# Shares of 24 and 8 token tiles instead of 16 and 16, and the results of six token groups loaded behind block 30 and summed between the last sends

## What is computed

```python
x = layernorm(x + attention(x))          # x: 16 x 256 tokens of 128; 16 heads of 8
x = layernorm(x + moe(x))
def moe(xf):                             # 4096 tokens
    shared = gelu(xf @ Wfc_s + bfc_s) @ Wproj_s + bproj_s      # hidden 512
    probs = softmax(xf @ Wr)             # 8 experts
    p, i = top_k(probs, 2); p = p / sum(p)
    routed = sum over the two: (gelu(xf @ Wfc[e] + bfc[e]) @ Wproj[e] + bproj[e]) * p
    return shared + routed
```

## Time and profile before

| what | us |
|---|---|
| median of three runs (590.12, 590.47, 601.82) | 590.47 |
| the profiled execution, its own time | 595.96 |
| its span, first to last instruction | 594.2 |
| attention part, up to | 279 |
| shared expert with routing and slot sends, up to | 403 |
| blocks 0 to 38, last result send ends at | 554.8 |
| sums, moments, normalisation, writing out, up to | 594.2 |

### The profile page before, as it was taken

The page is one execution under the profiler, slowest core; times in us unless marked ns, Lnnn a source line. Parts: engine busy times, 40 slices in busy tenths (PEclk is TensorE's granted clock), DMA queues, the critical chain, the costliest instruction groups (busy, mean ns, idle before and its releaser), DMA issues.

```text
span 594.2 us, 13730 instructions
## 1 busy us (share of the span) xinstructions
PE 436.2 (73%) x4871; PEld 280.8 (47%) x4871; DVE 364.2 (61%) x783; ACT 330.6 (56%) x624; POOL 327.2 (55%) x433
## 2 busy tenths in 40 slices
PE   5999999999999999984514530588989898897000
PEld 2344545555555554542303320367877687776000
DVE  3658887878787878762414710565666575664292
ACT  1148887878788888741424410564655565554043
POOL 5312676565666867437771677001655486675493
PEclk9889999999999999995756965799999999999555
DMA  3224535363645452011113111910111111000542
GB/s 89 65 63 119 154 101 154 111 156 100 174 143 154 135 145 66 30 37 40 54 54 95 34 54 54 242 34 1 38 40 35 38 36 31 30 26 29 191 160 73
DMA packets 63109, 50.25 MB, mean 85 GB/s; under 512 B 7338, under 2 KB 54580, under 8 KB 63044
## 3 DMA queue, kind: packets, MB, share of 16 engines
q1 hardware_dynamic: 58500, 40.91, 24.2%
q0 software_dynamic: 4544, 8.47, 4.3%
HBM read 24.96 MB, written 22.95 MB: 81 GB/s over the span
## 4 chain that ended last, share of the span: by engine, by line
PE 17%; another core or an unknown queue 13%; DVE 8%; ACT 6%; issue 5%; DMA 1%; POOL 1%; ACTq 0%; DVEq 0%; POOLq 0%; SPq 0%
ACT hid L1635 3%; PE h_ps L1565 2%; PE y_ps L1585 2%; PE h_ps L1566 2%; PE h_ps L1567 2%; PE y_ps L1586 2%; PE y_ps L1584 2%; ACT hid L1622 2%; DVE hid L1687 1%; DVE stats L1738 1%; DVE x_all L1735 1%; DVE var_eps L1743 1%; PE t_ps L1554 1%; ACT hid L1627 1%
## 5 line engine op out<-in xcount | busy, mean ns | idle before, releaser
L553 DVE TENSOR_REDUCE row_max<-s_ps 128x2 f32<-128x512 f32 x256 | 164.9, 683 | 49.8 <-PE s_ps L684 47.9
L413 ACT ACTIVATE probs<-ring_ps 128x1024 f32<-128x1024 f32 x128 | 130.9, 1023 | 49.0 <-PE ring_ps L702 48.6
L1481 POOL DMA_INDIRECT results<-gated,rows_in x78 | 89.8, 1151 | 93.3 <-ACT gated L1643 77.6
L684 PE MATMUL s_ps<-qk_stack 24*128 24x256 f16 x512 | 84.0, 272 | 7.8 <-DVE row_max L553 2.6
L702 PE MATMUL ring_ps<-qk_stack 26*128 26x256 f16 x512 | 83.0, 271 | 0.0
L1334 POOL DMA_INDIRECT slots<-rows,slot_at x64 | 63.7, 995 | 34.3 <-issue 19.2
L1635 ACT ACTIVATE hid<-h_ps,bias 128x256 f32<-128x256 f32 x156 | 61.3, 480 | 32.8 <-PE h_ps L1567 20.0
L720 PE MATMUL av_ps<-probs,v_aug 128*32 128x256 f32 x1024 | 68.5, 385 | 0.0
L684 PEld LDWEIGHTS s_ps<-qk_stack 24*128 24x128 f16 x512 | 34.3, 92 | 62.3 <-issue 32.8
L1585 PE MATMUL y_ps<-w,hid 128*128 x312 | 59.5, 220 | 1.7 <-issue 1.6
L1622 ACT ACTIVATE hid<-h_ps,b_units 128x512 f32<-128x512 f32 x32 | 21.9, 685 | 69.5 <-remote 59.3
(11 more groups left out here) (209 smaller groups left out, 1034.9 us busy)
## 6 DMA issues: line engine op xcount, KB each, us to landing
qk_stack<-qk_rows SPq DMA_DIRECT2D x64, 96.0 KB
slots<-empty_row SPq DMA_DIRECT2D x13, 390.0 KB, 5.2
qk_rows<-qk_parts SPq DMA_DIRECT2D x16, 256.0 KB, 2.6
rows<-results SPq DMA_DIRECT2D x8, 512.0 KB, 6.8
rows_in<-slots SPq DMA_DIRECT2D x3, 1300.0 KB, 10.8
w_stage<-in_w_fc SPq DMA_DIRECT2D x9, 256.0 KB, 3.3
w_stage<-in_w_proj SPq DMA_DIRECT2D x9, 256.0 KB, 3.8
x_t<-in_x_t SPq DMA_DIRECT2D x16, 128.0 KB, 2.2
```

Source lines behind the costliest of these rows:

```text
L413: nc.scalar.activation(probs[:, n % PROBS], ring(key), ACT.Exp, scale=SCORE_SCALE).then_inc(ring_emptied, 1)
L553: nc.vector.tensor_reduce(row_max[:, h], s1_ps[:, h % 2], AX_X, ALU.max, negate=True).then_inc(max_done, 1)
L684: mm = nc.tensor.matmul(s1_ps[:, h % 2, t], band_of(q_stack, b, h, TERM_ROWS)[:, t * P:(t + 1) * P], band_of(k_stack, b, h, TERM_ROWS), st ...
L1481: nc.gpsimd.indirect_dma_start(out=a["results"][:, :], out_offset=bass.IndirectOffsetOnAxis(ap=rows_in[:, 2 * n + half, DEST:DEST + 1].bit ...
```

## The change

The shares become 24 and 8 tiles. With them the Placer sends 48 rows of tiles for the first share and 16 for the second; the blocks that are surely full are 17 instead of 9, and the first share's tokens lie in blocks 0 to 30 (`EARLY_BLOCKS` = 31). Eleven of the thirteen emptying DMAs, not eight, are waited for ahead of the first share (`FIRST_TILES` 66). SP waits for the sends of blocks 0 to 30 and loads the results of groups 0 to 5, then waits for all and loads those of groups 6 and 7. POOL sums group g behind its sends of block 33 + g. Behind the last send and the sixth sum it takes one inverse root over the 24 columns of six groups, and then works on groups 6 and 7 as before. VectorE, behind its last block, takes the moments of groups 0 to 5, makes their six shifts, and then goes on with groups 6 and 7.

```diff
@@ -30,7 +30,7 @@
-SHARES = ((0, 16), (16, 32))
+SHARES = ((0, 24), (24, 32))
@@ -897,8 +897,11 @@
-FIRST_TILES = 48
+FIRST_TILES = 66
 FULL_BLOCKS = TOP * SHARES[0][1] // 2 - (EXPERTS - 1)
+EARLY_BLOCKS = TOP * SHARES[0][1] // 2 + EXPERTS - 1
+EARLY_GROUPS = SHARES[0][1] // GROUP
+SUM_AT = {EARLY_BLOCKS + 2 + g: g for g in range(EARLY_GROUPS)}
@@ -1383,7 +1386,7 @@
-        minus_half2 = sb("minus_half2", [P, GROUP])
+        minus_half2 = sb("minus_half2", [P, EARLY_GROUPS, GROUP])
@@ -1463,8 +1466,12 @@
             for buf in range(RING):
+                sp.wait_ge(sent[buf], 32 * times_sent(buf, EARLY_BLOCKS))
+            for g in range(EARLY_GROUPS):
+                load_results(g)
+            for buf in range(RING):
                 sp.wait_ge(sent[buf], 32 * times_sent(buf, SLOT_BLOCKS))
-            for g in range(GROUPS):
+            for g in range(EARLY_GROUPS, GROUPS):
                 load_results(g)
@@ -1487,19 +1494,23 @@
-            def invert_root(g):
+            def invert_roots(lo, hi):
                 pool.wait_ge(half_made, 1)
-                pool.wait_ge(totals, TOTAL_STEPS * (g + 1))
-                nc.gpsimd.tensor_tensor(rstd2[:, g], var_eps2[:, g], minus_half2[:], ALU.pow).then_inc(scale2_done, 1)
+                pool.wait_ge(totals, TOTAL_STEPS * hi)
+                nc.gpsimd.tensor_tensor(rstd2[:, lo:hi], var_eps2[:, lo:hi], minus_half2[:, 0:hi - lo], ALU.pow)\
+                  .then_inc(scale2_done, hi - lo)
...
             for n in range(SLOT_BLOCKS):
                 send_result(n)
-            sum_experts(0)
-            for g in range(GROUPS):
+                if n in SUM_AT:
+                    sum_experts(SUM_AT[n])
+            invert_roots(0, EARLY_GROUPS)
+            sum_experts(EARLY_GROUPS)
+            for g in range(EARLY_GROUPS, GROUPS):
                 if g + 1 < GROUPS:
                     sum_experts(g + 1)
-                invert_root(g)
+                invert_roots(g, g + 1)
@@ -1789,9 +1800,13 @@
-            for g in range(GROUPS):
+            for g in range(EARLY_GROUPS):
                 find_moments(g)
-                if g >= 1:
+            for g in range(EARLY_GROUPS):
+                make_shift(g)
+            for g in range(EARLY_GROUPS, GROUPS):
+                find_moments(g)
+                if g > EARLY_GROUPS:
                     make_shift(g - 1)
             make_shift(GROUPS - 1)
```

## The result

| | kernel before | changed kernel |
|---|---|---|
| median of 20 runs each | 597.29 us | 586.90 us (583.97 to 594.35) |
| the profiled execution, own time (span) | 595.96 (594.2) | 592.53 (590.8) |
| ratio of the runs | | 0.9873, 95% interval 0.9833 to 0.9914 |

A forecast was written before the change was run, and what follows sets the result against it. No engine was seen as the bound; time could come from POOL's rows of slot sends and the tail. Middle -1.5, contention +1.5 and tail -8.0 gave -8.0: 590.47 to 582.5 us, 8-in-10 range 573 to 590.

The forecast's parts named there:

- The middle: Attention-part routing, slot sends and shared units up to the block loop: together -1.5 us, between -12 and +4.
- so here too 18 units are begun at its end: Second row of slot sends: 18 shared units begun when it ends, as before, so only the rest of the hold is saved.
- +4 if three units fewer are done at release: Upper end for the middle: 4 us lost if three fewer shared units are done when the second row's hold ends.
- +0.7: Attention part: VectorE's first-share routing widens from 128x128 to 128x192, costing 0.7 us, between 0 and +1.5.
- first rival: Gap between the two slot-send rows closes, middle -10 instead of -1.5, kernel at 574 us; chance 0.14.
- Held until about 4 us behind the last send: Slot sends: a row holds the shared units of other engines until about 4 us after its last send.
- The early load: SP's six loads behind block 30's sends are in by 540; no sum waits, 4 us of cover.
- third rival: Early load lands late, at 551 instead of 534, holding POOL's sums and sends: +12.4, kernel at 595 us; chance 0.09.
- The sums between the sends: POOL's sums among the last result sends: last send ends 3.8 us later, plus 1.5 for contention with VectorE's halving.
- second rival: POOL's sums and VectorE's halving shut each other out and the root is dear: 589.9 or 586 us; chance 0.24.
- Root and normalisations: Tail: one inverse root over 24 columns takes 3.8 us, then ScalarE's 32 normalisations take 12.7 us.
- The end: Behind ScalarE's last normalisation: the 7.15 us to the end of the span stay as before.

The follow-up runs named there:

- e1: Kernel before with only the shares changed to 24 and 8 tiles, old end of the kernel kept; 592.07 us, ratio 0.9972 to the kernel before.
- e3: Changed kernel with the six early sums moved behind the last result send; 595.32 us, ratio 1.0002 to the kernel before.
- e4: Changed kernel with the inverse root taken over five groups, then over the sixth alone; 585.57 us, ratio 0.9862 to the kernel before.
- e8: The changed kernel itself, run again on chip D; 586.52 us, ratio 0.9923 to the kernel before.
- e2: Changed kernel with shares of 16 and 16 again, so four groups are loaded and summed early; 581.42 us, ratio 0.9800 to the kernel before.
- e7: e2 with the root moved off POOL: square root on ScalarE, reciprocal on VectorE; 581.08 us, ratio 0.9701 to the kernel before.
- e5: Changed kernel with POOL waiting at every slot send from the sixth on until the send before has landed; 611.99 us (one run).
- e6: Changed kernel with POOL waiting for the previous send to land only up to the 24th slot send; 583.69 us, ratio 0.9750 to the kernel before.
- e9: e10's kernel repeated on chip D; 574.13 us, ratio 0.9755 to the kernel before.
- e0: The kernel before, unchanged, run again on chip B for a second trace; 601.79 us (one run).
- e10: Changed kernel with POOL waiting at every second slot send from the sixth on, chip C; 554.45 us, ratio 1.0634 to the kernel before.
- e11: Changed kernel with shares of 20 and 12, e7's root and e10's wait, chip C; 548.45 us, ratio 1.0531 to the kernel before.

## Why the prediction was right, and where it wasn't

*The middle* (forecast -1.5, measured +4.2 at the first result send). The step that failed is "so here too 18 units are begun at its end". I had read unit 17's start, 21 us into the second row, as a property of the row; it was what the units had reached before it. With the long row ahead 14 had begun (15 in e1, e3, e4 and e8; 18 or 19 in the four traces with 16/16). The bound I wrote down for that, "+4 if three units fewer are done at release", is what came, in part by luck: unit 31 came 5.0 us later after the row's start, the first result send 1.4 more, and the row happened to start 2.2 us earlier. Of the +0.7 that I had for the wider routing ahead of it nothing is to be seen: the row starts at 277.1 to 278.9 in five traces with 24/8 and at 276.7 to 282.5 in four with 16/16. The hold was read rightly in that the rows touched in no trace of the change and the second share's counts lay behind the first row (unit 7 by 6.0 us), and the first rival (the gap closes) is out on these chips. "Held until about 4 us behind the last send" was too simple: unit 6 was let go 6 us ahead of the row's end, and in e2 and e7 unit 18 came 11.6 and 6.3 us ahead of that of the second. e5, e6 and e9 show that the hold ends when the sends stand apart; on chip C it may well not exist, and there the first rival's premise isn't tested.

*The early load* (forecast: no wait). Right: none of the six sums waited for its load in the profile after, nor in e8's. The third rival is out.

*The sums between the sends* (forecast +3.8 and +1.5 for contention). Measured +5.0 together, and 24.3, 23.9 and 24.3 us for this stretch in after, e4 and e8 against 19.2, 18.0 and 19.6 in before, e0 and e1. The size was right. It is paid by POOL rather than VectorE: a send directly behind a sum takes 1.27 to 1.80 us instead of 0.98. One halving took 2.62 us for 1.23, about a sum's 1.3 us more, as the second rival has it, but as that rival's "against" said, VectorE had time (its last halving ends at 551.8, its moments of group 4 wait for POOL).

*Root and normalisations* (forecast 3.8 and 12.7). Measured 4.21 and 12.41. From the last send to the last normalisation 20.4 us were forecast and 21.6 measured.

*The end* (forecast: the 7.15 us behind the last normalisation stay). Measured 2.7. This term I had copied without asking what it consisted of: before, it was POOL's drain behind its last root, and not the write of the output. Since the change ends POOL's work 2.5 us earlier and its drain is 1.3 us shorter, it is over before SP's work and no longer sets the end. e2, e4 and e7 show the drain as a bound of its own: it sets the end in the first two and not in the third.

*What remains* (+2.5 between the first result send and block 33). Scatter: the stretch is 118.7 to 124.1 us over the nine traces of both layouts with close slot sends on A, B, D and the result's, and 121.4 in before, 124.1 in e0.

So the errors were +5.7, -0.3, +1.2, -4.4 and +2.5, together 4.7 us, for the 4.6 between the span forecast (586.2) and that measured (590.8). These are the errors against one pair of executions, which differ by 3.4 us and not by the 7.5 of the means. Averaged over the traces named here, the first result send comes 3.7 us later with 24/8 (five traces against four), the blocks up to 33 take 1.6 less, which is scatter, the sends with sums 5.4 more, and the tail and the end 10.7 and 4.5 less as above: together -7.7, near the 7.5. So the ratio was met because the middle, 5.2 us dearer than forecast, and the end, 4.4 cheaper, nearly cancelled; that is luck. The absolute forecast of 582.5 lay 4.4 below the median of 586.9; it leaned on a median of three runs, 590.47, which twenty runs put at 597.3.

A version that beats both kernels is e7 (0.9701 on chip B, where the changed kernel itself didn't run; shares of 16 and 16, four groups early, no root on POOL). e7's edits with the pause at every second send were not tried on such a chip, and none of the versions but e10 and e11 ran on one like C.

## What to carry to other kernels

When rows of indirect sends stand beside other engines' work, look at whether the units go on under them, and how many are done when a row ends, before moving the row: a longer first row moved the standstill and lost three to four units. Put an engine's bulk work between its sends rather than behind them where another engine reads the same memory, and look up what the last microseconds of a span consist of: an engine's drain is hidden only if that engine is done early. And time a variant that trades send rate for less standstill on more than one chip: the same pause gained about 2% on the changed kernel on one and stood 6% above the kernel before on another.

## What was unexpected of the hardware

- Chips differ by kind here: the kernel before took 592.8, 598.0, 589.8 and 520.9 us on four of them. One kernel (e9, e10) ran its spaced part alike on two of them and its block loop in 138.1 and 121.6 us; TensorE was busy for 65.9 and 79.2 of the same 80 us. What sets the chips apart is open.
- Under close indirect sends of GpSimd (one each 1.3 us) ScalarE waited for TensorE's results by up to 26 us at a time, on chips A, B and D and in the two profiles of the result, and for up to 8.5 us in the block loop of e9; beside one send each 2.6 us, or two and a pause of 1.6 us, no wait for a shared unit was over 5.0 us. On chip C a train of result sends from 405 to 527 us held nothing.
- GpSimd's drain at the end of the program took 8.8 us with shares of 24/8, 9.7 with 20/12 and 10.1 to 10.4 with 16/16. Why it depends on the shares is open.
- An add of VectorE beside six sums of GpSimd in a row took 6.59 us for 0.68.
- GpSimd's inverse root: 0.73, 1.0 to 1.4, 2.97 and 4.21 us for 2, 4, 16 and 24 columns.
